# Attention on one core: the logarithm of the softmax sums joins the maximum in the bias rows, and the division behind the weighing goes

## The reference

```python
x = x + 0.5 * ffn(layernorm(x))          # router, 64 experts, top 6, one shared expert
x = x + attention(layernorm(x))          # itself layernorm, Q K V, rotary, softmax, W_out, + input
x = x + 0.5 * ffn(layernorm(x))
# attention: B, S, D = 4, 512, 512; 16 heads of 32 channels
scores = einsum('bhqd,bhkd->bhqk', Q, K) / sqrt(32)
ctx = einsum('bhqk,bhkd->bhqd', softmax(scores), V)
```

## Time and profile before

| what | value |
| --- | --- |
| median of 3 runs | 1473.46 us (1468.86 to 1473.66) |
| the profiled execution, its own time | 1466.83 us |
| its span in the profile | 1464.9 us |
| mean granted clock of PE over the span | 0.91 |
| first bias transfer issued | 525.3 us |
| last bias transfer issued | 975.0 us |

### The profile page before, as it was taken

The page is one execution under the profiler, slowest core; times in us unless marked ns, Lnnn a source line. Parts: engine busy times, 40 slices in busy tenths (PEclk is TensorE's granted clock), DMA queues, the critical chain, the costliest instruction groups (busy, mean ns, idle before and its releaser), DMA issues.

```text
span 1464.9 us, 25891 instructions
## 1 busy us (share of the span) xinstructions
PE 1272.7 (87%) x10162; PEld 782.4 (53%) x10162; DVE 609.1 (42%) x1108; ACT 544.2 (37%) x1329; POOL 507.0 (35%) x413
## 2 busy tenths in 40 slices
PE   4999998899882788999999899979998998898890
PEld 4633776576651544654564455435432766666660
DVE  6883222212224556555654765541585122221220
ACT  1412111111102177876876887674211211111110
POOL 0032454545543633332222332200021455554454
PEclk9996999999995778999999899878996999999995
DMA  8985799999959543232542334211654799999967
GB/s 301 388 338 184 257 342 338 340 333 337 325 88 315 153 117 101 73 87 62 134 109 73 102 83 106 73 51 73 231 206 154 234 342 343 342 335 333 340 117 131
DMA packets 146201, 307.35 MB, mean 210 GB/s; under 512 B 17568, under 2 KB 50720, under 8 KB 146080
## 3 DMA queue, kind: packets, MB, share of 16 engines
q1 hardware_dynamic: 112704, 238.06, 48.3%
q0 software_dynamic: 23808, 57.69, 17.4%
q10 hardware_dynamic: 9568, 9.94, 2.0%
HBM read 222.54 MB, written 61.87 MB: 194 GB/s over the span
## 4 chain that ended last, share of the span: by engine, by line
PE 51%; DMA 25%; DVE 10%; issue 5%; ACT 4%; POOL 3%; DVEq 0%; SPq 0%; POOLq 0%; ACTq 0%
DMA out<-osb,tok 10%; DMA ya_d<-osb,tok 9%; PE ps L385 8%; PE ps L451 6%; PE ps L507 6%; PE ps L401 5%; PE ps L495 4%; PE ps L518 4%; DMA buf<-xn_d,tok 4%; PE ps L463 3%; PE ps L436 3%; PE ps L282 2%; ACT ps L703 2%; PE ps L368 1%; DVE osb L998 1%
## 5 line engine op out<-in xcount | busy, mean ns | idle before, releaser
L385 PE MATMUL ps<-bufT,gu 128*64 128x96 f32 x6144 | 303.0, 261 | 0.0
L385 PEld LDWEIGHTS ps<-bufT,gu 128*64 128x64 f32 x6144 | 292.5, 177 | 9.1 <-issue 2.0
L1067 DVE TENSOR_REDUCE Mx<-ps 128x1 f32<-128x512 f32 x256 | 168.8, 684 | 106.0 <-PE ps L463 105.5
L998 DVE TENSOR_SCALAR osb<-ps,gt 96x512 f32<-96x512 f32 x128 | 93.9, 745 | 259.8 <-PE ps L401 77.4
L661 ACT COPY bufT<-ps 128x384 f32<-128x384 f32 x128 | 60.9, 477 | 344.3 <-PE ps L368 344.0
L703 ACT ACTIVATE ps<-ps,Mx 128x512 f32<-128x512 f32 x256 | 171.5, 671 | 45.0 <-DVE Mx L1067 40.5
L401 PE MATMUL ps<-wd,h 64*96 64x512 f32 x768 | 180.4, 602 | 3.2 <-DVE osb L998 3.2
L729 ACT ACTIVATE PT<-ps 128x512 f32<-128x512 f32 x256 | 152.9, 604 | 68.8 <-PE ps L495 67.1
L1168 POOL DMA_INDIRECT buf<-xn_d,tok x128 | 127.8, 998 | 93.9 <-issue 59.6
L1213 POOL TENSOR_TENSOR t<-t,rp 128x512 f32<-128x512 f32 x32 | 41.0, 1282 | 252.0 <-DVE t L1052 250.2
L495 PE MATMUL ps<-St 98*128 98x512 f32 x256 | 122.1, 488 | 5.7 <-ACT PT L729 5.7
(11 more groups left out here) (148 smaller groups left out, 1510.1 us busy)
## 6 DMA issues: line engine op xcount, KB each, us to landing
gu<-in_L_ffn_w_gate SPq DMA_DIRECT2D x64, 768.0 KB, 13.4
gu<-in_L_ffn_w_up SPq DMA_DIRECT2D x64, 768.0 KB, 15.8
wd<-in_L_ffn_w_down SPq DMA_DIRECT2D x64, 768.0 KB, 18.3
St<-HL SPq DMA_DIRECT2D x192, 128.0 KB, 2.3
wqk<-wp_d SPq DMA_DIRECT2D x32, 512.0 KB, 5.6
xn_d<-XN SPq DMA_DIRECT2D x24, 256.0 KB, 2.1
X<-in_L_attn_X SPq DMA_DIRECT2D x4, 1024.0 KB, 10.5
ya_d<-X SPq DMA_DIRECT2D x4, 1024.0 KB, 15.3
```

The source lines that it names most:

```text
L385: t = e.matmul(bk[64 * k:64 * k + 64, CAP * j:CAP * j + CAP], gu[:, 2 * k + m, c, j:F:3], f.bufT[(2 * q + k) % 4][:, c, :], start=(c == 0) ...
L998: e.tensor_scalar(f.osb[x % 4][:, :], bank(4 + x % 2)[0:CAP, :], f.gt[:, x % 8:x % 8 + 1], None, ALU.mult).then_inc(f_ev, 1)
L1067: e.tensor_reduce(Mx[:, qt, hl:hl + 1], bank((4, 5, 7)[n % 3]), AX, ALU.max, negate=True).then_inc(a_max, 1)
```

## The change

`Dn` is no longer inverted. ACT takes its logarithm into `Ln` (`act_log`, slot 14, behind the exponential of tile 11), DVE subtracts it from the negative maximum into `Ls` (`dve_lse`, slot 14), and `pe_rows`, now in slot 15, turns `Ls` round instead of `Mx`. The copy and the split of the rows (`act_rows`, `dve_rows`) and the transfers (`fill`, now on SP) move to slot 0 of the next turn. The second pass then yields probabilities that are already divided, and the whole path of the division goes. The third weighing moves from slot 14 to slot 0 of the next turn.

```diff
-        def pe_spread(e, u):
...
-        def pe_broadcast(e, u):
...
         def pe_rows(e, u):
-            e.wait_ge(a_max, 16 * u + 16)
+            e.wait_ge(a_lse, u + 1)
             bk = turn(e, ("mh", u), a_mhl, u + 1)
             for qt in range(4):
-                t = e.transpose(bk[0:4, 128 * qt:128 * qt + 128], Mx[:, qt, :], ident)
+                t = e.transpose(bk[0:4, 128 * qt:128 * qt + 128], Ls[:, qt, :], ident)
...
-                e.wait_ge(a_nrm, 4 * b + 4)
+                e.wait_ge(a_dr, 4 * b + 4)
...
-        P_AT, S_AT, V_AT, T_AT, W_AT = (0, 1, 3, 4), (3, 6), (8, 9, 11, 13), (5, 8, 10, 12), (7, 12, 14)
+        P_AT, S_AT, V_AT, T_AT, W_AT = (0, 1, 3, 4), (3, 6), (8, 9, 11, 13), (5, 8, 10, 12), (7, 12)
...
-                    if back and j == 1:
-                        pe_spread(e, u - 1)
-                    if back and j == 4:
-                        pe_weigh(e, u - 1, 3)
-                    if back and j == 6:
-                        pe_broadcast(e, u - 1)
+                    if back and j in (0, 4):
+                        pe_weigh(e, u - 1, 2 + j // 4)
...
-                    if nxt and j == 13:
+                    if nxt and j == 15:
                         pe_rows(e, u + 1)
...
-        def act_spread(e, u):
-            e.wait_ge(a_tr, u + 1)
+        def act_log(e, u):
+            e.wait_ge(a_den, 16 * u + 16)
             if u:
-                e.wait_ge(a_bc, u)
-            e.copy(rd[:, :], bank(has["rd", u])[0:4, :]).then_inc(a_rd, 1)
+                e.wait_ge(a_lse, u)
+            e.activation(Ln[:, :, :], Dn[:, :, :], ACT.Ln).then_inc(a_log, 1)
...
-                    if nxt and j == 13:
-                        act_rows(e, u + 1)
                     if nxt and j == 14:
-                        act_fill(e, u + 1)
+                        act_log(e, u + 1)
+                    if now and j == 0:
+                        act_rows(e, u)
...
-        def dve_invert(e, u):
...
-        def dve_broadcast(e, u):
...
+        def dve_lse(e, u):
+            e.wait_ge(a_log, u + 1)
+            if u:
+                e.wait_ge(a_rows, u)
+            e.tensor_tensor(Ls[:, :, :], Mx[:, :, :], Ln[:, :, :], ALU.subtract).then_inc(a_lse, 1)
...
-                    if nxt and j == 13:
-                        dve_rows(e, u + 1)
-                    if nxt and j == 15:
-                        dve_invert(e, u + 1)
+                    if nxt and j == 14:
+                        dve_lse(e, u + 1)
+                    if now and j == 0:
+                        dve_rows(e, u)
...
+        def fill(e, u):
+            e.wait_ge(a_mhl, u + 1)
+            if u >= 3:
+                e.wait_ge(a_ST, 16 * (u - 2))
+            for j in range(2):
+                e.dma_start(St[u % 3][96 + j:97 + j, 0, :, :].bitcast(F32), mh[:, j, :].bitcast(F32)).then_inc(s_m[u % 3], 16)
...
+                    if j == 0 and 0 <= u < NU:
+                        fill(e, u)
```

More of the change, by code:

```diff
@@ L37 @@
 NP = 8
-C_ID, C_LM, C_IE, C_TK, C_HD, C_N = 0, 128, 192, 256, 272, 400
+C_ID, C_LM, C_IE, C_TK, C_N = 0, 128, 192, 256, 272
 def shape_constants():
@@ L49, in shape_constants @@
     c[:, C_TK:C_TK + 16] = T - (np.arange(NT)[None, :] * 128 + p[:, None])
-    c[:4, C_HD:C_HD + 128] = p[:4, None] == p[None, :] // DH
     rot = DH // 2
@@ L127, in macaron_kernel @@
         xF = at("xF", o + 10 * KB, [128, 4, 128])
-        rd = at("rd", o + 12 * KB, [4, S])
         o += 14 * KB
         Dn = at("Dn", o, [128, 4, 4])
-        Rn = [at("Rn", o + 64 * (j + 1), [128, 4, 4]) for j in range(2)]
+        Ln, Ls = [at("Ln", o + 64 * (j + 1), [128, 4, 4]) for j in range(2)]
         Mx = at("Mx", o + 192, [128, 4, 4])
@@ L153, in macaron_kernel @@
         a_Vmm, a_V, a_P, a_shuf, a_rot, a_cos, a_qk = [sem("a_" + x) for x in ("Vmm", "V", "P", "shuf", "rot", "cos", "qk")]
-        a_hi, a_lo, a_sc, a_max, a_den, a_inv = [sem("a_" + x) for x in ("hi", "lo", "sc", "max", "den", "inv")]
-        a_tr, a_rd, a_bc, a_nrm = [sem("a_" + x) for x in ("tr", "rd", "bc", "nrm")]
+        a_hi, a_lo, a_sc, a_max, a_den, a_log, a_lse = [sem("a_" + x) for x in ("hi", "lo", "sc", "max", "den", "log", "lse")]
         a_rows, a_mhh, a_mhl = [sem("a_" + x) for x in ("rows", "mhh", "mhl")]
@@ L464, in pe_scores @@
                      start=True, stop=True).then_inc(a_sc, 1)
-        def pe_spread(e, u):
[L467 to L471, removed]
-        def pe_broadcast(e, u):
-            e.wait_ge(a_rd, u + 1)
-            bk = turn(e, ("nrm", u), a_nrm, u + 1)
-            e.matmul(bk, cst[0:4, C_HD:C_HD + 128], rd[:, :], start=True, stop=True).then_inc(a_bc, 1)
         def pe_rows(e, u):
-            e.wait_ge(a_max, 16 * u + 16)
+            e.wait_ge(a_lse, u + 1)
             bk = turn(e, ("mh", u), a_mhl, u + 1)
             for qt in range(4):
-                t = e.transpose(bk[0:4, 128 * qt:128 * qt + 128], Mx[:, qt, :], ident)
+                t = e.transpose(bk[0:4, 128 * qt:128 * qt + 128], Ls[:, qt, :], ident)
             t.then_inc(a_rows, 1)
@@ L700, in act_scores @@
             e.wait_ge(a_max, n + 1)
-            if j == 0 and u:
-                e.wait_ge(a_inv, u)
             e.activation(bk, bk, ACT.Exp, bias=Mx[:, qt, hl:hl + 1], accum_out=Dn[:, qt, hl:hl + 1]).then_inc(a_den, 1)
-        def act_spread(e, u):
-            e.wait_ge(a_tr, u + 1)
+        def act_log(e, u):
+            e.wait_ge(a_den, 16 * u + 16)
             if u:
-                e.wait_ge(a_bc, u)
-            e.copy(rd[:, :], bank(has["rd", u])[0:4, :]).then_inc(a_rd, 1)
+                e.wait_ge(a_lse, u)
+            e.activation(Ln[:, :, :], Dn[:, :, :], ACT.Ln).then_inc(a_log, 1)
         def act_rows(e, u):
@@ L715, in act_rows @@
             e.copy(mh[:, 0, :], bank(has["mh", u])[0:4, :]).then_inc(a_mhh, 1)
[L717 to L722, removed]
         def act_expo(e, u, j):
@@ L757, in act_attention @@
                         act_split(e, u + 2, S_AT.index(j))
-                    if back and j == 1:
-                        act_spread(e, u - 1)
                     if back and j == 4:
@@ L1064, in dve_scores @@
             if j == 0 and u:
-                e.wait_ge(a_rows, u)
+                e.wait_ge(a_lse, u)
                 e.wait_ge(a_den, 16 * u)
             e.tensor_reduce(Mx[:, qt, hl:hl + 1], bank((4, 5, 7)[n % 3]), AX, ALU.max, negate=True).then_inc(a_max, 1)
-        def dve_invert(e, u):
[L1070 to L1073, removed]
-        def dve_broadcast(e, u):
-            e.wait_ge(a_bc, u + 1)
-            e.wait_ge(a_dr, u + 1)
-            e.tensor_tensor(cT[:, u % 4, :], cT[:, u % 4, :], bank(has["nrm", u]), ALU.mult).then_inc(a_nrm, 1)
+        def dve_lse(e, u):
[3 more added lines that the diff above has]
+            e.tensor_tensor(Ls[:, :, :], Mx[:, :, :], Ln[:, :, :], ALU.subtract).then_inc(a_lse, 1)
         def dve_rows(e, u):
@@ L1097, in dve_attention @@
             for u in range(-2, NU + 1):
-                nxt, far, back = 0 <= u + 1 < NU, 0 <= u + 2 < NU, 0 <= u - 1 < NU
+                now, nxt, far = 0 <= u < NU, 0 <= u + 1 < NU, 0 <= u + 2 < NU
                 new, val = new_tiles(u), new_values(u)
@@ L1111, in dve_attention @@
                         dve_value(e, j - 8)
-                    if back and j == 6:
-                        dve_broadcast(e, u - 1)
                     if j == 3:
```

## The result

The changed kernel takes 1494.9 us, the median of 4 runs (1487.4 to 1506.4), against 1473.5 for the kernel before: a ratio of 1.0158, with a 95% interval of 1.0109 to 1.0208. It is slower, by 1.1 to 2.1%. (The ratio is the one on record; the quotient of the two medians is 1.0145, inside the interval.) Measured once more beside the last experiments it has 1.0165 (1.0133 to 1.0197). Some executions of a kernel are slower than the rest, and medians and ratios here leave them out: one of the kernel before at 2959 us, one each of e1 (1483.1) and e4 (3863), and three of the thirteen of e10 (1470.8 to 1476.9). The profiled execution took 1487.4 us against 1466.8, so 20.6 us more, and these can be placed: from the first score matmul of the attention to the first matmul of the shared expert in turn 16 (L299 before, L296 after) it is 520.3 us before and 540.3 after (499.8 to 1040.07).

What follows compares the result with a forecast made beforehand. PE was taken to bound slots 0 to 4 and, with value tiles, from 8 on, ACT slots 5 to 7. Seam terms +8.4 +9.0 -3.6 +4.8 -2.2 gave +16.4 us: 1490 from 1473.5, range 1461 to 1513.

Steps and rivals of the forecast that it cites:

- late bias rows: Start of a turn: rows land 6.5 us after the transposes end, making slot 3 2.1 us late in turns with values.
- The loads: Around the logarithm on ACT: two table loads a turn, 1.28 us each; with the logarithm 2.8 us, 16 times, 45 us.
- behind values: Seams after the 6 turns with value tiles: +1.4 us each, +8.4 us in all.
- behind new tiles and turns -1 and 0: Seams after 5 turns with nothing on PE at the end to cover the chain: +1.8 us each, +9.0 us.
- behind results: Seams after turns 4, 8, 12, where the last result on PE covers the loads: -1.2 us each, -3.6 us.
- behind 13 and 14, and the end: Turns 13 and 14, whose next turn has no projection: +4.8 us; turn 15 and the end, without logarithm: -2.2 us.
- bank 1: Projection's second half: PE's wait of 0.46 us a turn goes, as it now follows the bias rows in bank order.
- ACT's gap: Slots 5 to 7, where ACT is the bound: its gap of 0.28 us after the weighed sum's copy comes back.
- the clock as a rival: PE's new waits lower its clock in 9 turns: 22 us more, 1512 us; chance 0.20.
- the weighing's wait: Seam between turns: PE's 0.83 us wait in the third weighing for tile 11's exponential goes.
- One table and rows in time: Rival: no loads in the turns and bias rows landing in time, -26 us, 1447 us; chance 0.12.
- One table and late rows: Rival: no loads in the turns but bias rows still late, -4.4 us, 1469 us; chance 0.05.

Runs made afterwards that it cites:

- e1: The changed kernel, with ACT told once to load the table that holds exp and ln, after the last root of the attention's start: 1470.6 us, ratio 1.0004.
- e4: The kernel before, with only the third weighing moved to slot 0 of the next turn: ratio 1.0037.
- e10: The changed kernel with one table, bias rows first in slot 0, last bias transfers ahead of SP's loads, and the third weighing back in slot 14: 1455.1 us, 0.9895.
- e3: The changed kernel, with turn 15's two bias transfers started ahead of SP's wait and five weight loads: 1489.1 us, ratio 1.0118.
- e12: The changed kernel as it stands, measured once more against the kernel before: ratio 1.0165.
- e11: The kernel before, with the division left out (inversion, transposes of Rn, spreading matmul, copy, product on cT), output not divided: ratio 0.9932.
- e6: The kernel before, with the third weighing in slot 0 of the next turn and the bias transfers on SP in slot 14: ratio 1.0027.
- e7: The changed kernel with one table for exp and ln, bias rows first in slot 0, and last bias transfers ahead of SP's loads: ratio 0.9926.
- e9: The changed kernel, with the third weighing back in slot 14: 1516.8 us, ratio 1.0298.

## Why the prediction was right

**The sum.** 16.4 us were forecast and 20.6 measured in the profiled executions (1490 against 1494.9 by the medians). The mechanism held: loads, late transposes, late bias rows, a late slot 3. That the sum came so near is in part luck, as the list of what was mis-sized shows.

**The loads** came as read from the earlier trace rows: two a turn of 1.28 us, 2.81 us from tile 11 to tile 12 (645.71 to 648.53), with 0.02 us between an exponential and a load. The drain that the Trainium skill, "ScalarE: Activation LUTs", section "What ACT_TABLE_LOAD costs", counts besides doesn't show in any of the 32. Its section "Table sets: the hidden batching unit" is right that one set serves exp and ln: the changed kernel doesn't get it by itself, while e1, which asks for it, has no load beside the logarithm.

**The seam** in the turn with values, shifted by the 8.00 us: end of the transposes forecast 647.95, measured 648.10; transfers 651.55 and 651.48; first matmul of the second pass 654.45 and 654.42. The price of 2.3 us for the landing, taken from a 128 KB transfer, fits the 8 KB one: 2.94 us from the first issue to the matmul, where 0.6 + 2.3 was forecast. At the first weighing, slot 7, the delay was 1.58 us (662.13 - 644.22 against 652.55 - 636.22), where 1.4 was forecast.

**What was mis-sized,** by the list of seams:

| seams | forecast | measured |
| --- | --- | --- |
| behind values, 6 | +8.4 | +12.2 |
| behind new tiles and turns -1 and 0, 5 | +9.0 | +12.1 |
| behind results, 3 | -3.6 | -5.9 |
| behind 13 and 14, and the end | +4.8 - 2.2 | +3.2 - 1.5 |

(1) Values: +2.0 each, not +1.4. Slot 3 was 2.05 us late (654.42 - 8.00 - 644.37), as forecast, and 0.74 us was to come back (0.46 for bank 1, 0.28 for ACT's gap). At the full clock the turn is still 1.8 late at its next score tile 15, so only 0.2 came back; why was not tried. The lower clock at three of the six seams adds 0.4 each, some 1.2 us of the 3.8. The prediction had the clock as a rival of 22 us more; behind values it came in that small part, and for the other seams it was not told apart. (2) Turn 15: the prediction priced `fill` on SP at nothing, since "`fill` is through well before slot 6". In turn 15 SP's wait and five loads stand ahead of it; that is some 3 us (e3). (3) Behind new tiles it is +0.9 to +3.1 where +1.8 was forecast; behind results -1.3 and -1.4 where -1.2 was forecast, but -3.2 at the third, into turn 13. Neither was tried. (4) The last part, behind 13 and to the end, is 1.7 us with the 3 us of `fill` in it, where 2.6 was forecast without them. But in e12, the same kernel, it is 7.6 us longer than in the profiled execution of the change, so one execution does not fix its size. The seams behind values and new tiles and the missing term make 10 us more than the sum had, the rest 6 us less, and that is the luck in it.

**The terms for what goes.** The prediction listed 3.0 us a turn of PE's work and waits that go. e11 says that the division alone is worth 0.6 us a turn in the kernel before, and e4 and e6 that the weighing's wait of 0.83 us and the transfers' 1.21 us on ACT's queue are worth nothing. In the sum the division stood with 0.46 + 0.28 us behind slot 3, of which 0.2 came back as told in (1); the transposes' 0.55 did not count, since the bias rows set slot 3.

**The rivals.** "One table and rows in time" gave 1447; e7 is that kernel, with the last transfers mended too, and has 0.9926, 1462 us. It was priced too low mostly at the seams behind new tiles (forecast -3.8 us, measured +6.8), where the move of the weighing to slot 0 costs; behind results it is -6.2 where -11.5 was forecast, behind values -4.6 where -6.9 was. "One table and late rows" gave 1469, and e1 has 1.0004, 1470.6 us; its parts agree less well, with +8.6 behind new tiles where 2.5 was forecast.

## What to carry to other kernels

In this kernel a function that was not in the loaded table cost two loads each time it stood alone between others. Ask for a table that holds both, and if there is none, put it where nobody waits for it, since the same 41 us of loads took 22 us from one kernel and 4 us from another. When work is moved to another queue or slot, go through the special turns as well as the regular one: the last turn had a wait of its own ahead of the place to which the transfers were moved. And read a change by kind of turn before calling it worth nothing: the third weighing in slot 0 won behind results and lost behind new tiles.

## What was not expected of the hardware

PE's granted clock fell from 1.00 to 0.70 of full speed in the 5 us behind a wait of 2.15 us in which it had nothing left to do (e9), and work of 1.54 us took 2.43. In the changed kernel it fell to 0.73 around a wait of 2.19 us before the transposes at one seam (617 to 622 us), and stayed at 1.00 at another behind a wait of the same 2.19 us and one of 0.98 (645 to 662 us). e12 repeats the lengths of all six such turns to 0.2 us and shows the lower clock at the same three seams (0.77, 0.72 and 0.72 over 6 us each), so in these two executions the same seams fell. What decides between the two was not found.
